# Recurrent attention with a gated ternary feed-forward: one cast buffer, a sixth weight slot, transposes in another order and PSUM half

## The reference

```python
xn = layernorm(x)                                # over 2048 features
q, k, v = xn @ Wq + bq, xn @ Wk + bk, xn @ Wv + bv   # 16 heads of 128
qf, kf = elu(q) + 1, elu(k) + 1
# chunks of 128 tokens; per head
kv = einsum('chd,che->hde', kf, v)               # one chunk
inter = qf @ (sum of kv of the chunks before);  z_inter = qf . (sum of kf before)
A = tril(qf @ kf.T);  intra = A @ v;  z_intra = A.sum(-1)
s = ((inter + intra) / (z_inter + z_intra + 1e-6)) @ Wo + bo
xn2 = layernorm(xn) * ln_w + ln_b
Wt = clip(round(W / mean(|W|)), -1, 1)           # ternary weights
y = x + s * silu(xn2 @ Wt)
```

## Time and profile before

| | us |
|---|---|
| median of 2 runs | 3929.7 |
| the two runs | 3888.06, 3971.35 |
| the profiled execution | 3890.33 |
| its span, slowest core (core 6 of 8) | 3888.5 |
| spans of the 8 cores | 3858.4 to 3888.5 |
| granted TensorE clock, mean | 0.849 to 0.853 |

### The profile page before, as it was taken

How to read it: one execution, slowest core, us unless ns; L and a number is a source line. 1 busy time by engine, 2 the same in 40 slices (tenths; PEclk the granted TensorE clock), 3 DMA queues, 4 the chain that set the end, 5 groups by cost and what they waited for, 6 DMA issues and landing times.

```text
span 3888.5 us, 41502 instructions; the slowest of 8 cores (3858.4 to 3888.5 us)
## 1 busy us (share of the span) xinstructions
PE 2821.1 (73%) x15876; PEld 1462.8 (38%) x15876; DVE 979.1 (25%) x957; ACT 1218.4 (31%) x1712; POOL 217.0 (6%) x268
## 2 busy tenths in 40 slices
PE   1244445595978599687969597768969696959876
PEld 1011112443453344443444344334444344434443
DVE  3222354411221212311240222221141123121222
ACT  5001100514333342415242433324251433334321
POOL 2232112000000000000000000000000000000000
PEclk7577767797988799898989799879979798979988
DMA  6898868145413543145414542254414541444324
GB/s 212 265 289 281 277 217 279 67 146 179 152 60 114 190 142 119 56 155 176 154 40 136 178 152 82 94 177 155 137 37 147 182 153 45 129 133 154 105 85 132
DMA packets 133054, 581.64 MB, mean 150 GB/s; under 512 B 16000, under 2 KB 16096, under 8 KB 108288
## 3 DMA queue, kind: packets, MB, share of 16 engines
q1 hardware_dynamic: 105984, 436.25, 34.6%
q0 software_dynamic: 26880, 142.74, 10.6%
HBM read 503.43 MB, written 75.50 MB: 149 GB/s over the span
## 4 chain that ended last, share of the span: by engine, by line
PE 62%; DMA 13%; ACT 11%; DVE 7%; issue 6%; POOL 1%; DVEq 0%; ACTq 0%; SPq 0%; POOLq 0%
PE psA L485 53%; DMA wsc<-pcast 6%; ACT xn2T L453 3%; DMA y<-xres 3%; DMA wring<-wsc 2%; ACT scr L627 2%; ACT scr L632 2%; DMA xres<-x 1%; PE psB L429 1%; DVE qat L647 1%; PE psB L544 1%; PE psB L551 1%; POOL wsc L239 1%; PE psA L573 1%; DVE a_m L581 1%
## 5 line engine op out<-in xcount | busy, mean ns | idle before, releaser
L485 PE MATMUL psA<-xnT,wring 128*128 128x512 bf16 x6144 | 1419.8, 396 | 340.1 <-DMA wring<-wsc 339.6
L485 PEld LDWEIGHTS psA<-xnT,wring 128*128 128x128 bf16 x6144 | 618.2, 101 | 1138.5 <-issue 474.5
L485 PE MATMUL psA<-xn2T,wring 128*128 128x512 bf16 x2048 | 485.1, 403 | 93.9 <-ACT vg L682 48.5
L485 PE MATMUL psA<-qat,wring 128*128 128x512 bf16 x2048 | 443.3, 379 | 0.0
L485 PEld LDWEIGHTS psA<-xn2T,wring 128*128 128x128 bf16 x2048 | 209.3, 103 | 367.1 <-issue 152.2
L714 DVE TENSOR_TENSOR xnT<-scr,vg 128x512 bf16<-128x512 f32 x128 | 88.6, 692 | 807.3 <-ACT scr L706 807.3
L485 PEld LDWEIGHTS psA<-qat,wring 128*128 128x128 bf16 x2048 | 200.4, 98 | 241.6
L529 ACT ACTIVATE vg<-psA,bs_v 128x512 bf16<-128x512 f32 x128 | 88.0, 687 | 443.9 <-PE psA L485 443.9
L500 ACT ACTIVATE scr<-psA,bs_q 128x512 f32<-128x512 f32 x128 | 88.0, 687 | 443.6 <-PE psA L485 443.5
L500 ACT ACTIVATE scr<-psA,bs_k 128x512 f32<-128x512 f32 x128 | 88.0, 687 | 417.9 <-PE psA L485 417.9
L453 ACT ACTIVATE xn2T<-psB,lnb_sb,lnw_sb 128x128 bf16<-128x128 bf16 x512 | 182.1, 491 | 59.7 <-PE psB L435 59.7
(11 more groups left out here) (97 smaller groups left out, 2294.4 us busy)
## 6 DMA issues: line engine op xcount, KB each, us to landing
wring<-wsc SPq DMA_DIRECT2D x640, 512.0 KB, 3.8
wsc<-pcast POOLq DMA_DIRECT2D x160, 256.0 KB, 8.3
xln<-x POOLq DMA_DIRECT2D x32, 1024.0 KB, 10.0
xres<-w_f SPq DMA_DIRECT2D x32, 1024.0 KB, 7.7
xres<-x POOLq DMA_DIRECT2D x32, 1024.0 KB, 7.7
y<-xres POOLq DMA_DIRECT2D x32, 1024.0 KB, 7.6
xres<-w_q SPq DMA_DIRECT2D x16, 1024.0 KB, 6.4
xres<-w_k SPq DMA_DIRECT2D x16, 1024.0 KB, 7.3
```

The lines of the kernel that those rows point to most:

```text
L485: op("tensor", lambda e, k=k, ti=ti, bk=bk, rb=rhs_buf: e.matmul(psA[:, bk * 512:(bk + 1) * 512], wring[k % 5][:, ti * 128:(ti + 1) * 128] ...
```

## The change

- The ring `wring` has 6 slots instead of 5; a tile waits for the tile six back.
- `pcast` is one buffer, which both names stand for; each cast waits for the stores of both semaphores of its matrix, that is for the step before.
- In `emit_ln_B` the 16 transposes of `xns` come first, those of `kftok` or `vtok` second. The keys keep their meaning.
- The transposes of step 5 go to banks 0 and 1 of `psA` (as bf16) instead of the lower half of `psB`, wait for these banks, and the residual add releases them.

```diff
-        NRING = 5
+        NRING = 6
-        pcast = [e_(nc.sbuf_tensor(f"pcast{i}", [128, D], CDT)) for i in range(2)]
+        pcast0 = e_(nc.sbuf_tensor("pcast0", [128, D], CDT))
+        pcast = [pcast0, pcast0]
...
+        psAT = psA.ap().bitcast(BF16)
...
                 cslot = pcast[sl]
-                cr = cast_rel[sl]
-                if cr is not None:
-                    wait("vector", cr[0], cr[1])
+                for cr in cast_rel:
+                    if cr is not None:
+                        wait("vector", cr[0], cr[1])
...
-            if k >= 5:
-                wait("sync", s_wfree, k - 4)
+            if k >= 6:
+                wait("sync", s_wfree, k - 5)
...
                 wait_rel("tensor", "psB")
                 for t in range(NT):
                     incs = [(s_pe, 1)] if t == NT - 1 else []
+                    op("tensor", lambda e, t=t, xm=xnstm: e.transpose(
+                        psBT[:, 2048 + t * 128:2048 + (t + 1) * 128],
+                        xm[:, t * 128:(t + 1) * 128], identb[:, :]), incs)
+                pe_tr2 = s_pe.n
+                for t in range(NT):
+                    incs = [(s_pe, 1)] if t == NT - 1 else []
                     op("tensor", lambda e, t=t, xm=xntm: e.transpose(
                         psBT[:, t * 128:(t + 1) * 128],
                         xm[:, t * 128:(t + 1) * 128], identb[:, :]), incs)
                 pe_tr1 = s_pe.n
-                for t in range(NT):
-                    incs = [(s_pe, 1)] if t == NT - 1 else []
-                    op("tensor", lambda e, t=t, xm=xnstm: e.transpose(
-                        psBT[:, 2048 + t * 128:2048 + (t + 1) * 128],
-                        xm[:, t * 128:(t + 1) * 128], identb[:, :]), incs)
-                pe_tr2 = s_pe.n
...
             for j in range(NCH):
                 c = sc * NCH + j
-                wait_rel("tensor", "psB")
+                for bk in range(2):
+                    r0 = psA_bank_rel[bk]
+                    if r0 is not None:
+                        wait("tensor", r0[0], r0[1])
                 for t in range(NT):
                     wait("tensor", s_dv, dv_sg[t])
                     incs = [(s_pe, 1)] if t == NT - 1 else []
                     op("tensor", lambda e, t=t, j=j: e.transpose(
-                        psBT[:, t * 128:(t + 1) * 128],
+                        psAT[:, t * 128:(t + 1) * 128],
                         xnT[:, t * T + j * 128: t * T + (j + 1) * 128],
                         identb[:, :]), incs)
...
                 op("vector", lambda e, sl=sl: e.tensor_tensor(
                     xres[sl][:, :].rearrange("p (t d) -> p t d", d=128),
-                    psBT_lo3d(),
+                    psAT[:, 0:2048].rearrange("p (t c) -> p t c", c=128),
                     xres[sl][:, :].rearrange("p (t d) -> p t d", d=128),
                     ALU.add), [(s_dv, 1)])
                 dv_out = s_dv.n
-                set_rel("psB", (s_dv, dv_out))
+                psA_bank_rel[0] = (s_dv, dv_out)
+                psA_bank_rel[1] = (s_dv, dv_out)
```

More of the change, by code:

```diff
@@ L51, in build_nc @@
     prog = {k: [] for k in ("sync", "gpsimd", "scalar", "vector", "tensor")}
-    s_w = [Sem(f"w{i}") for i in range(5)]
+    s_w = [Sem(f"w{i}") for i in range(6)]
     s_xl = [Sem(f"xl{i}") for i in range(2)]
@@ L302, in stream_wtile @@
             op("sync", lambda e, m=m, to=to, k=k: e.dma_start(
-                out=wring[k % 5][:, :].rearrange("p (t d) -> p t d", d=128),
-                in_=wsc[MIDX[m], to, :, :, :]), [(s_w[k % 5], 16)])
-            return k, (s_w[k % 5], s_w[k % 5].n)
+                out=wring[k % 6][:, :].rearrange("p (t d) -> p t d", d=128),
+                in_=wsc[MIDX[m], to, :, :, :]), [(s_w[k % 6], 16)])
+            return k, (s_w[k % 6], s_w[k % 6].n)
         def load_xln(c):
@@ L486, in proj_phase @@
                             psA[:, bk * 512:(bk + 1) * 512],
-                            wring[k % 5][:, ti * 128:(ti + 1) * 128],
+                            wring[k % 6][:, ti * 128:(ti + 1) * 128],
                             rb[:, ti * T:(ti + 1) * T],
```

## The result

The changed kernel takes 4099.1 us in the median of 11 runs, the kernel before 3891.9 in the median of 10: ratio 1.0544, 95% interval 1.0499 to 1.0588, slower. The profiled execution has 4098.4 us, its slowest core (core 1) a span of 4096.8. In some runs of nearly every kernel here one die or both were slower at a lower granted clock; ratios, and the times of the experiments, are those of the other runs, by which the change costs 209 us (medians 4098.2 and 3888.9).

The account below looks back on a forecast made before the run. Load, cast, store was taken to bound the prologue, TensorE the token groups. Terms 177 + 59 + 0 - 29 + 2 = +209 us on 3890.3 gave 4099 us; 4002 to 4197 held 0.69, 3987 to 4227 8 in 10.

Parts of the forecast that it names:

- The bound: Whole kernel: a prologue of some 660 us paced by load, cast, store, then seven token groups of some 425 us set by TensorE.
- P = 2.75 + L with L = 6.3: Period of a converting step: 2.75 us plus the second half store's landing, taken as 6.3; about 9.0 us, casts +177 us.
- The one interval over the first tile: Between 16th and 17th cast, over q stores, first weight tile, projection and evacuation: 19.9 us becomes 22.
- the ternary steps: 16 converting steps after the sums, before attention: 7.05 us a step becomes 11.6, over 13 intervals +59 us.
- The loop through TensorE: Prologue weight tile, projection, evacuation, next cast: 17.2 us against three periods or 27 us; 10 us to spare, no share in period.
- The 16 sums: Absolute sums between casts and ternary steps, 450 to 545 us: they use no cast buffer, so nothing changes.
- The sixth slot: Sixth slot of the weight-tile ring: worth 0, since no tile waits for a slot, and takes nothing away.
- The passages: Seven changes from one token group to the next: 4.2 us saved each by both transpose edits, 29 us in all.
- The four pieces: Per passage: start 7.6 us earlier, rounds 0 and 1 each 1.65 longer, round 2 1.55 earlier, round 3's copy 1.65 later.
- Stores are quick: Rival: store landing nears 3.7 to 4.2 us, so not slower; 3904 us at 3.7; chance 0.10.
- The estimate of 2.6 us for a bare store: Skill page's landing for 256 KB, 2.0 us plus bytes over 436 GB/s: some 3821 us; chance of a gain 0.02.
- A landing that stays at 8.3: Rival: store landing keeps its old median 8.3 us despite halved stores, +359 us, 4249 us; chance 0.15 for above 7.6.

## Why the prediction was right, and where its terms were not

**The bound.** That the prologue goes by load, cast, store and the groups by TensorE held: the buffer changed only the stretch to 925 us (one buffer alone +239), the transposes only what comes after.

**The step with one buffer.** P = 2.75 + L with L = 6.3 was the term that mattered. The first 16 casts went at 8.76 (41.40 to 172.84 in 15 steps), so L was 6.0 there; in the projections 47 steps took 444.1 us (192.06 to 636.16), 9.45 each, so L was 6.7. The one interval over the first tile became 19.2 instead of 22. The choice was made for a store beside one load; the weight tile that joins every second step was left out of it. This is the mis-sized term: +191.5 measured for +177 (+187 in the mean of the cores). The same holds in the ternary steps, 155.8 / 13 = 12.0 a step where I had 11.6, and +62.3 for +59.

**The loop through TensorE.** It was said to have room, and has: VectorE's waits before the casts are put down to the store for 62 of 64, and without the loads, at steps of 6.5 to 6.9 us, still for 60.

**The 16 sums.** "Nothing" was wrong by 9.3 us on the two cores of the table and by 4.7 in the means, to the good. The stretch has no store in it. Its pairs take 10.1 us (653.32 to 713.97 in six pairs) where they took 11.2 before (462.93 to 529.85, also six); the tiles in it are seen below. Why the stretch settled in another rhythm was not tested.

**The sixth slot.** 0 predicted, and five slots in its place make no difference that shows.

**The passages.** The four pieces measure as predicted: start 7.6 earlier relative to the last add (5.2 before it instead of 2.4 behind), first two rounds +1.7 each, third -1.55, and q 1.5 later in the last. That is 4.2 a passage; 34.5 instead of 38.7 from the last add to q. The stretch after attention began gave 38.2 us on the two cores of the table and 36.6 in the means of eight, not 29. In the same means both transpose edits alone give 33.9 and the one buffer alone 1.7; psA alone gives 56.9 where 53 were expected, and the exchange alone costs 25.7 where 24 were. So most of the excess comes with the transposes in psA. Its cause stays open: the time from the first to the last residual add, 179.3 us in the seven passages before and 174.4 after, is 184.2 with psA alone and doesn't account for it.

**The rivals.** Stores are quick only when there is no load: 3.7 in the median without the loads. With the load kept, the first 16 steps have a median of 5.9 and the steps beside projections 6.5. The estimate of 2.6 us for a bare store (the Trainium skill, DMA: Bandwidth & Descriptors, Anatomy of one DMA) was not reached in any run; the least is 3.3. A landing that stays at 8.3 fell too: 6.2 over all stores. (That rival's ternary step should read 13.6 us, 11.6 + 2.0, and not 14.2; its sum is not touched.)

**Luck in the choice of L.** The right number came from a row that stands for something else. The two stores with 6.4 to 6.6 us were taken for one step's stores with weight tiles and no load. But GpSimd issued six loads of 1 MB for the next group right behind them (four from 659.34, two from 661.48 us), and the transfer engines were busy all the time (share 1.03), where they are 61% busy in the steps of the changed kernel (columns as in the earlier trace rows):

```profile
655.00:666.00 11.00, 11.00 (x53) 5.00 (x51) 1.93 (x2) 2.06 (x3) 4.96 (x8) 1.00 1.03 309
```

The last four stores of the changed kernel, of which the last two have the same six loads issued behind them, met transfer engines that were busy for 0.64 of the time (900 to 914 us) and 0.48 (914 to 920), and landed far sooner:

```profile
DMA to landing us min/median/max: 3.5/3.8/3.8
```

So no row of before showed one step's stores beside a single load. That 6.3 was near the 6.0 and 6.7 is luck in part; taking a value between the quiet 3.7 and the crowded 8.3 was the sound half of the choice.


## What to carry to other kernels

Before taking a buffer from a chain of load, convert and store, write its period with one buffer as instruction times plus one landing, and take that landing from rows with the traffic that will be in flight then, counting the transfers that join every second step. How much a further buffer can still give shows in the busy share of the transfer engines: here it was 61% with one buffer, 87% with two and 92% with three, and the third gave some 34 to 43 us where taking the second away cost 239. When a PSUM half is changed to let the next stage start early, leave the order of the blocks so that the engine that sets the stage's pace gets what it waits for first: here the move alone gave 60 us and the exchanged order took half of it back.

## What was not expected of the hardware

In the stretch of the 16 sums TensorE's tiles of 16 matmuls took 5.3 to 6.1 us and 3.61 us in turn, while before they took 4.9 to 6.6 throughout. Timeline of TensorE alone, after:

```profile
653.51 3.61 PE L487 MATMUL psA<-xnT,wring 128*128 128x512 bf16 x16 [2.32 <-DMA wring<-wsc]
665.65 5.67 PE L487 MATMUL psA<-xnT,wring 128*128 128x512 bf16 x16 [8.52 <-DMA wring<-wsc]
673.80 3.61 PE L487 MATMUL psA<-xnT,wring 128*128 128x512 bf16 x16 [2.48 <-DMA wring<-wsc]
```

The three quick tiles began after 2.3 to 3.2 us idle and ran at the higher clock, 2.4 GHz: the granted clock is 1.00 over the first of them (653.00 to 657.20 us). Those after 7 us idle or more took 5.3 to 6.1; over the second row the granted clock is 0.63 in the mean (665.60 to 671.40), so about three quarters of that time passed at the lower level, 1.2 GHz. One tile after 2.96 us idle took 5.00, so the gap alone does not decide. Before the change the gaps were 4.1 to 6.3 us, and no tile was quick. It bears only on the stretch of the sums, 4.7 to 9.3 us shorter, where it may be part of the cause; that was not tested.

GpSimd's issue of a store took 0.89 us in the median in both kernels, but up to 1.72 before and up to 0.91 after; with one buffer no cast runs while a store is being issued. The Trainium skill (SBUF — State Buffer, SBUF: two separate sides) says that a VectorE operation of this kind keeps GpSimd from writing descriptors, and these rows agree. It gave back 20 us of GpSimd's time (217.0 to 196.5). An issue lies between a cast and its landing, so part of this may count in a step; how much was not tested.
